# Attention and FFN block on one core: batch 0 first, maxima 12 slots ahead, shift rows on ACT's queue

## What is computed

```python
def fake_quant_fp8(t):
    amax = jnp.max(jnp.abs(t))
    scale = FP8_E4M3_MAX / jnp.maximum(amax, 1e-12)
    q = (t * scale).astype(jnp.float8_e4m3fn).astype(jnp.float32)
    return q / scale
...
    scores = jnp.einsum('bhqd,bhkd->bhqk', Qr, Kr) * DH ** (-0.5)
    causal = jnp.triu(jnp.ones((t, t), dtype=bool), 1)
    scores = jnp.where(causal[None, None], neg, scores)
    pattern = jax.nn.softmax(scores, axis=-1)
...
x = L0_attn_X
xn = _layernorm(x, axis=-1)
x = x + attn(xn) @ W_o.T + (einsum('bsd,od->bso', fake_quant_fp8(xn), fake_quant_fp8(weight)) + bias)
```

## Time and profile before

| | us |
|---|---|
| median of 3 runs (lowest to highest) | 467.93 (467.34 to 469.64) |
| the profiled execution | 468.62 |
| its span | 466.9 |

### The profile page before, as it was taken

How to read it: one execution, slowest core, us unless ns; L and a number is a source line. 1 busy time by engine, 2 the same in 40 slices (tenths; PEclk the granted TensorE clock), 3 DMA queues, 4 the chain that set the end, 5 groups by cost and what they waited for, 6 DMA issues and landing times.

```text
span 466.9 us, 9145 instructions
## 1 busy us (share of the span) xinstructions
PE 405.5 (87%) x2819; PEld 222.8 (48%) x2819; DVE 350.1 (75%) x1340; ACT 277.3 (59%) x500; POOL 274.4 (59%) x278
## 2 busy tenths in 40 slices
PE   1790676999889999999999999999999999998975
PEld 1440521364345556654565556555655545643443
DVE  3779899969769977997799778977897878842041
ACT  2742932147765677567666765677567656675850
POOL 2304376636746984698459844985498337226552
PEclk9996555599999999999999999999999999999999
DMA  7826747300483238422851375037504760020021
GB/s 234 257 87 197 159 136 193 81 5 18 143 214 84 69 101 204 131 69 78 216 144 46 93 213 152 32 110 206 158 18 124 194 170 2 4 93 3 1 91 46
DMA packets 37617, 53.43 MB, mean 114 GB/s; under 512 B 5152, under 2 KB 31136, under 8 KB 37536
## 3 DMA queue, kind: packets, MB, share of 16 engines
q1 hardware_dynamic: 37568, 52.84, 40.6%
HBM read 35.78 MB, written 17.04 MB: 113 GB/s over the span
## 4 chain that ended last, share of the span: by engine, by line
PE 44%; POOL 22%; ACT 11%; issue 10%; DVE 8%; DMA 3%; POOLq 1%; SPq 1%; ACTq 0%; DVEq 0%
PE st_ps L842 10%; PE o_ps L922 9%; PE s_ps L860 7%; ACT prob L722 6%; PE m_ps L894 5%; PE m_ps L869 4%; POOL prob L427 4%; POOL rot L259 4%; PE m_ps L798 4%; POOL rot L253 3%; DVE scratch L587 3%; POOL xq L457 3%; POOL parts L263 3%; POOL rot L252 2%; POOL qv L453 2%
## 5 line engine op out<-in xcount | busy, mean ns | idle before, releaser
L587 DVE CUSTOM_DVE_ANT_0 scratch<-s_ps,causal 128x512 bf16<-128x512 f32 (+3 forms) x512 | 220.9, 485 | 55.0 <-PE s_ps L860 52.9
L722 ACT ACTIVATE prob<-st_ps 128x512 f32<-128x512 f32 x320 | 174.8, 600 | 97.9 <-PE st_ps L842 97.4
L427 POOL TENSOR_SCALAR_AFFINE_SELECT prob<-prob 128x512 f32<-128x512 f32 (+1 forms) x160 | 86.4, 544 | 130.9 <-ACT prob L722 129.4
L860 PE MATMUL s_ps<-k_st,q_st 96*128 96x512 bf16 (+3 forms) x512 | 130.8, 320 | 7.0 <-DVE rowmax L587 3.2
L842 PE MATMUL st_ps<-q_st,k_st 98*128 98x128 bf16 (+3 forms) x512 | 121.9, 303 | 4.2 <-ACT prob L722 2.8
L922 PE MATMUL o_ps<-prob,v_sb 128*17 128x512 f32 (+3 forms) x1024 | 87.4, 437 | 10.0 <-ACT heads L737 5.1
L842 PEld LDWEIGHTS st_ps<-q_st,k_st 98*128 98x128 bf16 x512 | 42.0, 97 | 76.3 <-ACT prob L722 42.3
L860 PEld LDWEIGHTS s_ps<-k_st,q_st 96*128 96x128 bf16 x512 | 48.9, 99 | 43.7 <-DVE rowmax L587 20.6
L922 PEld LDWEIGHTS o_ps<-prob,v_sb 128*17 128x17 f32 x1024 | 20.5, 96 | 48.3 <-issue 36.0
L587 DVE DVE_READ_ACCUMULATOR2_ANT rowmax<- 128x1 f32 x512 | 41.7, 81 | 0.1
L894 PE MATMUL m_ps<-wo_sb,attnT 128*128 128x256 f32 x128 | 33.2, 381 | 1.8 <-DVE x_res L610 1.4
(11 more groups left out here) (99 smaller groups left out, 502.6 us busy)
## 6 DMA issues: line engine op xcount, KB each, us to landing
qk_parts<-parts SPq DMA_DIRECT2D x16, 768.0 KB, 3.7
q_st<-qk_parts SPq DMA_DIRECT2D x32, 192.0 KB, 3.3
k_st<-qk_parts SPq DMA_DIRECT2D x32, 192.0 KB, 3.7
q_st<-x_dram SPq DMA_DIRECT2D x8, 512.0 KB, 5.5
q_st<-qk_parts SPq DMA_DIRECT2D x32, 128.0 KB, 3.4
k_st<-qk_parts SPq DMA_DIRECT2D x32, 128.0 KB, 3.7
x_res<-x_dram SPq DMA_DIRECT2D x8, 512.0 KB, 3.5
out_dram<-x_res SPq DMA_DIRECT2D x8, 512.0 KB, 4.8
```

Source lines behind the costliest of these rows:

```text
L427: eng.affine_select(out=ap, in_=ap, compare_op=ALU.is_ge, fill=0.0, base=0, pattern=pat, channel_multiplier=-1).then_inc(masked, 1)
L587: eng.tensor_tensor_reduce(scratch[:, at, col:col + w], s_ps[at][:, col:col + w], causal[:, T - w:T], 1.0, NEG, ALU.add, ALU.max, rowmax[: ...
L722: eng.activation(prob[u][:, half * T:(half + 1) * T], st_ps[ST_BANK[2 * s + half]][:, :], ACT.Exp, scale=SCALE).then_inc(exp_done, 1)
L860: mm = eng.matmul(bank[:, col:col + (qb + 1) * P], q_st[0:ROWS, 1 - par, h, qb * P:(qb + 1) * P], k_st[0:ROWS, 1 - par, h, 0:(qb + 1) * P] ...
```

## The change

- The raw x is loaded into `xnT` itself and normalised and transposed in place, so that the stacks of batch 0 don't share memory with it. Batch 0 is normalised, projected, split into parts (in halves) and written first; batches 1 and 2 follow, and batches 3 to 7 are normalised, transposed and copied inside the slots -11 to -2 (`TURN_SLOT`), with their statistics ahead of them or at slots -10 and -7.
- One list of slots from -12 to 178 takes the place of the iterations. Maxima run `LEAD` = 12 slots ahead of exponents. `OFFSETS` gives the slot of each small step relative to its batch's slot 0; projections stand at -32 to -25 and no longer at -39 to -34.
- The eight amplitude reductions are at the odd slots 1 to 15 of batch 0, the weights' quantisation at slots 16 to 21.
- Maxima are turned and split for each group of four heads (four times 16 rows a batch and not twice 32). ACT issues two transfers for each group straight from `shift` to `q_st`, two slots after the split and four before the first use, and DRAM is left out. The stack reads on SP are for eight heads each.
- The output of the last batch is stored in four pieces. Finish of block 3 stands one slot earlier.

```diff
+LEAD = 12
...
-MISC = [(0, "mt", 1), (0, "v", 0), (1, "qk", 0), (2, "qk", 1), (3, "v", 1), (4, "qk", 2), (5, "o", 0),
...
+OFFSETS = {("v", 0): 0, ("v", 1): 3, ("o", 0): 23, ("o", 1): 24, ("mt", 2): 4, ("o", 2): 25, ("o", 3): 26,
...
+TURN_SLOT = {3: -11, 4: -9, 5: -7, 6: -5, 7: -2}
...
-        xnT = sb("xnT", [P, NC, NB * T])
+        xnT = sb("xnT", [P, NB, NC, T])
...
-            def shift_rows(n, par, half_):
-
-                eng.wait_ge(shift_done, 2 * n + half_ + 1)
-                eng.dma_start(shift_dram[half_].rearrange("t a n -> a t n"), shift[:, :, :])\
-                   .then_inc(shift_out[half_], 16)
-                eng.wait_ge(shift_out[half_], 16 * (n + 1))
...
+            def store(n):
+                to = out[n].rearrange("(n p) d -> p n d", p=P)
+                if n < NB - 1:
+                    eng.wait_ge(fin_done, 4 * n + 4)
+                    eng.dma_start(to, x_res[:, :, :]).then_inc(y_out, 16)
+                else:
+                    for qb in range(NQ):
+                        eng.wait_ge(fin_done, 4 * n + qb + 1)
+                        eng.dma_start(to[:, qb, :], x_res[:, qb, :]).then_inc(y_out, 16)
...
+                if slot in (-10, -7):
+                    statistics({-10: 6, -7: 7}[slot])
+                if slot in range(1, 2 * NB, 2):
+                    largest(slot // 2)
+                weight_step(slot)
...
+            def shift_rows(n, g):
+
+                c = NG * n + g
+                eng.wait_ge(shift_done, c + 1)
+                for t in range(SHIFT):
+                    eng.dma_start(q_st[ROWS + t:ROWS + t + 1, n % 2, g * HG:(g + 1) * HG, :],
+                                  shift[:, t, :]).then_inc(shift_in[c % 2], 16)
```

More of the change, by code:

```diff
@@ new lines, with schedule @@
+SPREAD = [(17, "spread", 0, 0), (18, "spread", 0, 1)]
+TURN_SLOT = {3: -11, 4: -9, 5: -7, 6: -5, 7: -2}
+def schedule():
+    order = {key: i for i, key in enumerate(OFFSETS)}
+    items = [(SLOTS * n + off, order[kind, k], kind, n, k) for (kind, k), off in OFFSETS.items() for n in range(NB)
+             if (kind, n) != ("qk", 0)]
+    items += [(slot, len(order), kind, n, k) for slot, kind, n, k in SPREAD]
+    return [(slot, kind, n, k) for slot, _, kind, n, k in sorted(items)]
+SHARED = schedule()
@@ L53, with shared_at, exponent_slot @@
+SHARED_BANK = {item[1:]: i % 2 for i, item in enumerate(SHARED)}
+FIRST_SLOT, END_SLOT = -LEAD, SLOTS * NB + 19
 HALVES = 2 * SLOTS
 ST_BANK = [i % 2 for i in range(HALVES)]
-ST_BEFORE = [max(j for j in range(-HALVES, i) if ST_BANK[j % HALVES] == ST_BANK[i]) for i in range(HALVES)]
+ST_BEFORE = [i - 2 for i in range(HALVES)]
+def shared_at(slot, *kinds):
+    return [item[1:] for item in SHARED if item[0] == slot and item[1] in kinds]
+def exponent_slot(slot):
+    n, s = divmod(slot, SLOTS)
+    return (n, s) if 0 <= n < NB else None
@@ new lines, in maximum_slot, with batch_at, quant_at @@
+def maximum_slot(slot):
+    return exponent_slot(slot + LEAD)
+def batch_at(slot, offset, first=0):
+    n, rest = divmod(slot - offset, SLOTS)
+    return n if rest == 0 and first <= n < NB else None
+QUANT_STEPS = ("qv", "qe", "qc", "qw", "xq")
+def quant_at(slot, step):
+    k = QUANT_STEPS.index(step)
+    first, last, loop = (23, 24, 25, 26, 28), (16, 17, 18, 19, 20), (16, 17, 21, 22, 24)
+    return [n for n in range(NB) if SLOTS * n + (first if n == 0 else last if n == NB - 1 else loop)[k] == slot]
@@ L61, in wait_past @@
         eng.wait_ge(sem, count)
[L64 to L68, removed]
 def unit_parts(u, half):
@@ L231, in attention_ffn_block @@
         reader = {"qk": (roped, 4), "v": (v_copied, 2), "o": (normed, 4), "at": (at_copied, 4),
[L232 to L239, removed]
+                  "fin": (fin_done, 4), "mt": (shift_done, 4)}
@@ L381, in _ @@
+            store(NB - 1)
+            eng.wait_ge(y_out, 16 * (NB - 1 + NQ))
         @block.gpsimd
@@ new lines, in high_x, with exp @@
+            def high_x(n):
+                wait_past(eng, full["qk"], 4 * n if n > 1 else 0)
+                eng.copy(x_parts[:, 0], xnT[:, n]).then_inc(x_high, 1)
+            def exp(n, s):
+                g, u = divmod(s, 5)
+                if n > 0 or g > 0:
+                    eng.wait_ge(pv_done, 12 * n + 3 * (g - 1) + (1, 1, 2, 2, 3)[u])
+                for half in range(2):
+                    eng.wait_ge(st_full, 2 * (SLOTS * n + s) + half + 1)
+                    eng.activation(prob[u][:, half * T:(half + 1) * T], st_ps[ST_BANK[2 * s + half]][:, :],
+                                   ACT.Exp, scale=SCALE).then_inc(exp_done, 1)
@@ new lines, in bank_free @@
+            def bank_free(item):
+                kind, n, k = item
+                at = [i[1:] for i in SHARED].index(item)
+                if at >= 2:
+                    kind, n, k = SHARED[at - 2][1:]
+                    if kind == "spread":
+                        eng.wait_ge(wquant, 1 + 2 * k)
+                    else:
+                        done, per = reader[kind]
+                        eng.wait_ge(done, per * n + k + 1)
+                else:
+                    eng.wait_ge(roped, at + 1)
```

1007 lines of the change are left out of this document (478 added, 529 removed).

## The result

The kernel takes 514.57 us in the median (513.75 to 517.06) against 468.33 (467.34 to 469.64) for the kernel before on the same chip: 1.099 times as long, 95% interval 1.095 to 1.104. The profiled execution took 514.65, its span is 512.9. The forecast was 447.8, so it is wrong in sign and by 67 us. Two of the later runs (both moves together; second reads six slots later) had one slow execution in four, which is in their medians and not in their ratios to the kernel before.

The account below looks back on a forecast made before the run. The prediction took PE to bound the loop, with 1.64 us left per batch. From 466.9, terms of -18.1, -3, +3.5 and -2.5 gave a 446.8 span, or 447.8 on the median; range 441 to 455, chance 0.61.

Parts of the forecast that it names:

- Bound of the kernel before: Loop: PE busy 45.56 of 47.2 us per batch, so removing every wait gains at most 1.64 us per batch.
- First term: Start: batch 0's first maxima come at about 37.5 us instead of 58.10; bounds 35 to 42.
- Second term: Start: twelve slots instead of twenty before the first exponent take 29 us, putting it at 66.5 instead of 90.45.
- the 74 from which it was called wrong: Start: a first exponent later than 74 us would show the forecast wrong, through ACT's ring or the clock.
- the half-clock rival: Start stays at half clock, set by PE: twelve slots cost 36 us instead of 29; 456 in all; chance 0.11.
- Third term: Batch 0 gets dearer: 49 us instead of 43.2, bounds 43.5 to 54; batch 1 begins at 115.5 instead of 133.65.
- DVE's sum: Batch 0: DVE's maxima, ropes, reductions, split maxima and weights' chain, plus about 2 us of waiting, sum to 49 us.
- Fourth term: Loop: moved POOL, ACT and DVE work saves 0.5 us a batch, 3 in all; bounds 9.8 gained to 2.4 lost.
- the landing, even at 6 us, costs nothing: Loop: PE needs the shift rows four slots, 9.4 us, after their issue, so a 6 us landing is free.
- the slower rival: Loop: shift-row issues hold ACT and delay exponents, deciding from 3.0 us a pair; 518 us; chance 0.05 with anything else slower.
- Fifth and sixth terms: Last batch: eight slots of maxima land there, +3.5 us; tail: earlier finish and output in four pieces, -2.5 us.
- another queue: Loop: SP's large transfers stay in a queue other than ACT's, an argument that shift-row issues take only 0.23 to 0.51 us.

Follow-up runs that it names:

- both moves together: Changed kernel with the residual's load at slot 20 instead of 23 and the bias add at slot 30 instead of 26: 495.18 us, 1.0545.
- the last experiment: Kernel of 477.61 us with each of eight amplitude reductions on DVE reading one sixteenth of its elements: 472.99 us, 1.0089.
- 477.6: Changed kernel with bias add at slot 30, second stack reads six slots later, second V copy one earlier, shift rows on SP, residual's load at 26: 477.61 us, 1.0163.
- the kernel of 482.2 us: The fastest version with the shift rows issued by ACT instead of SP: 482.15 us, 1.0295.
- the fastest version: Kernel of 477.61 us with the first query stack reads four slots earlier and the key stack read one slot earlier: 464.11 us, 0.9896.
- the two other moves: Second stack reads six slots later, on the late bias add: 489.68 us; residual's load at offset 26 instead of 23, with shift rows on SP: 477.61 us.

## Why the prediction was wrong

**Bound of the kernel before.** Right: PE with 1.64 us left. It should have been a warning: with so little slack every new wait shows in full, and there are eight batches to repeat it.

**First term, maxima at 37.5.** 39.1. Right.

**Second term, first exponent at 66.5.** 70.5, under the 74 from which it was called wrong: 31.4 us behind the first maxima where 29 was forecast. From 39.0 to 68.2 DVE was busy 27.38 us of 29.2. The clock was mostly at its upper level (0.89 on the mean there), so the half-clock rival did not come. The Trainium skill (TensorE: Matmul & The Clock Gate, Part 4: PE-mode transpose) has it that matmuls in transpose mode do not count as busy for the clock in the way that others do. This stretch has other matmuls beside the transposes, so it can neither bear that out nor refute it.

**Third term, batch 0 in 49 and batch 1 at 115.5.** Batch 0 took 50.1 by the mark, 51.3 from exponent to exponent; batch 1 began at 121.8. The size was right to 2.3 us. The reason, DVE's sum, fits this kernel (busy 45.84 us where the sum had 47 and 2 of waiting), but the last experiment, on another version, does not bear it out, so it is not shown. Of the 18.1 us forecast by the first three terms 11.8 came.

**Fourth term, the loop.** Here it failed, in four steps.
1. *"casts, x parts, quantisation and bias add no longer meet in the same slots"*, bounded at 2.4 us lost. I read from the order what no longer met, and did not ask what meets now: load (slot 3), bias add (6), split of x (7), projection (8), each the cause of the next. 25.8 us hang on it by the run that moved the bias add. Two smaller meetings were missed in the same way: the second copy of V ahead of the turned heads (about 7 us) and the first reads of the query stacks beside the write of the keys' parts (about 13 us from 477.6 to 464.1). The load's landing, 3.5 us before, was not costed at all, although it had moved into the reads of stacks. The bound of 2.4 rested on no row.
2. *"the landing, even at 6 us, costs nothing"*. Pairs issued beside the burst took about 9 us. And the margin was not four slots: the pair issued at 393.91 was wanted by PE at 399.2 (403.13 less 3.90), 5.3 us later, since PE works ahead of the slot's exponents. In the changed kernel PE waits 6.1 us for such pairs; in the kernel of 482.2 us, where other stalls don't cover it, 12.4 us hang on SP's burst.
3. *"On ACT they add ... hidden as well"*, by 0.23 to 0.51 us each. They take 0.51 and 0.61, a pair 1.12, so four pairs 4.5 us of ACT a batch instead of about 3, and they cost 5.6 us of the time, less than a microsecond a batch. As the price of ACT alone the slower rival's point of decision, 3.0 us a pair, was never reached. That rival gave 518, near what was measured, but from another mechanism.
4. *"PE's instructions per batch stay (four transposes of 16 rows for two of 32)"*. A transpose of 16 rows took 273 ns here and one of 32 rows 272. The groups of PE in one batch, of before and of after:

```profile
L907 PE MATMUL m_ps<-ident,rowmax 128*32 128x128 f32 x2 | 0.5, 272 | 0.0
```

```profile
L887 PE MATMUL m_ps<-ident,rowmax 128*16 128x128 f32 x4 | 1.1, 273 | 0.4 <-DVE x_res L590 0.4
```

That is 0.6 us a batch and a wait of 0.4 more. In the fastest version PE is busy 46.64 against 45.56.

What this prediction did not look at is what SP does next. It told which transfers leave SP's queue and not that their waits leave with them. Before, 6.0 us pass between the two transfers and the load comes behind; after, no wait for maxima stands between the key reads, the load and the second reads. The other waits on SP (parts written, scores of an earlier batch done) did not hold them, as the burst at 286.95 to 290.25 shows.

**Fifth and sixth terms.** Forecast +3.5 and -2.5, so +1.0 from the last mark to the end; measured +1.4, and +0.2 in the fastest version. Right in their sum; whether each is right or two errors cancel, the mark can't tell.

**Where the rest of the gain is.** From the changed kernel to the fastest version 50.5 us were won: 25.8 with the bias add, about 7 with the copy of V, 6.5 with the shift rows on SP, about 13 with the query reads; the two other moves gave nothing clear of noise. The fastest version, 464.1, is still 16.3 us above the forecast, and its profiled execution, the slowest of five at 466.5, 18.0 by its span. By its marks batches 0 and 1 took 51.6 each, where 49 and 46.7 were forecast, and four more 48.3 each instead of 46.7: 2.6, 4.9 and 6.3, 13.8 in all. Its first exponent, at 71.6 instead of 66.5, came 5.1 later; together that is 18.9, near the 18.0. Batch 1's excess (clock 0.97, PE busy 48.3) was not traced further.

The Trainium skill (DMA: Bandwidth & Descriptors, "Issuing engines are not separate DMA queues") says that transfers started by different engines run on the same 16 DMA engines and interleave, so that a second issuing engine saves the sequencer's time alone. The traces agree: in the kernel of 482.2 us, 4 KB from ACT's queue took about 9 us beside SP's burst, where the median of all 64 such transfers is 1.7. The prediction had spoken of "another queue" as cover.

## What to carry to other kernels

Before moving work in a kernel whose engine has 3% left, write for each moved instruction who waits for it and what stands behind it on its engine; two steps that are harmless apart (a wait for a load, a split that a matmul needs) are a stall when one stands ahead of the other. A wait that is removed from a DMA-issuing engine may have been the one that spread its transfers in time; look where that engine is held once it is gone. And an edit that gives nothing while a larger stall is there isn't refuted: the same one was worth 2 (within noise), 6.5 and 18 us as the others were mended. It also did two things at once, since it took the issues off ACT and put waits on SP; of the 18 us, 12.4 came from the waits.

## What the runs showed of the hardware

A 512 KB load landed in 3.5 us in the median where it was issued apart from the reads of stacks (the kernel before, and the changed one with the load three slots earlier) and in 8.8 among them (the changed kernel). Transfers of 4 KB landed there in 1.6 us at least, 1.8 in the median and 10.6 at most. SP's place in the order of slots set no time: the second reads went out 5.9 us behind the batch's mark, and 19.8 us behind it with nothing changed but waits on SP. After a stall of 7.0 us PE ran at the lower clock for about 3 us though busy throughout (rows 206 to 209 above), and it did so behind the stall of 3.90 us too, in this stretch of that run:

```profile
404.00:406.00 2.00, 2.00 (x18) 0.50 (x16) 1.40 (x6) 0.72 (x2) 1.11 (x2) 0.50 0.01 4
```

Stalls of 0.4 to 0.6 us in the loop of the kernel of 464.1 us (4.1 us in all from 228 to 372) left its batches at 1.00.
